# The head of a fused state-space and gated-FFN kernel: factors over 128 partitions, two load queues, row tiles normalised one by one

## The chip, the cores and the metric

The kernel runs on one core of one Trainium2 chip, as one launch. The metric is device time in microseconds. The engines are TensorE (PE; its weight loads are PEld), VectorE (DVE), ScalarE (ACT), GpSimd (POOL) and SyncE (SP), which here only issues transfers.

## The reference, cut to what matters

```python
x  = L0_attn_u                        # (2, 1024, 512): 2048 rows of 512, float32
xn = layernorm(x)                     # over the 512, eps 1e-5
s  = causal_conv(xn, K) + D * xn      # K: 512 taps from the S4 parameters (a small chain of complex work)
def lora_linear(x, w, a, b):          # rank 16
    return x @ w.T + (x @ a.T) @ b.T * 2.0
h1 = lora_linear(xn, w1, A1, B1)      # 1376 hidden units
h3 = lora_linear(xn, w3, A3, B3)
g  = silu(lora_linear(silu(h1) * h3, w2, A2, B2))
out = x + s * g
```

## The kernel before

**Tiling.** The 2048 rows are four blocks of 512. For each block the 1376 hidden units are 11 tiles (`HT`) of up to 128; each tile j has three places: "gate" (h1), "up" (h3) and "down" (the product with w2 for tile j - 1). The weights stay in SBUF. In the first block each weight tile must first be made: it is loaded (`load_raw`), the rank-16 product of the factors is formed on PE into a spare bank (`fold`), DVE adds it (`fold_add`), ACT rounds the sum to the high part (`fold_hi`) and DVE or POOL subtracts to give the low part (`fold_lo`; the list `POOL_LO` says which tiles are POOL's). Every matrix product is three matmuls on high and low parts (`three`, lines 819 to 821).

**The head.** Before tile 1 of the first block, four row tiles of 128 rows are loaded into `xn`, their mean and variance are formed on DVE (`rows_moments`, lines 671 and 674), scale and shift on POOL (`rows_rstd`, two row tiles at a time), applied on ACT (`rows_norm`, line 559), turned on PE (`turn_rows`, line 814) and split by ACT and DVE (`rows_hi`, `rows_lo`, lines 533 and 678). Tile 0's h1 and h3 are made in halves of 256 rows, since the first two row tiles are ready first: `start()` on PE holds that order, with the first five folds (`FOLD_FIRST`) in between, and `keep_busy` matmuls on a cleared tile that give nothing. The first factors come as `lr`, 16 partitions by 2176 columns. All factors are also loaded as `spread` (128 partitions by 708), split by ACT and POOL and stored by six transfers as a stack of 48 rows over 128 partitions, which the folds from `(1, 2)` on read.

**What sets the order.** All engines run hand-written instruction lists in order; waits on semaphores join them. All loads are on SP's queue. The spare banks alternate between folds, and a fold waits until DVE has read the bank's last one. After the head, PE's list for tile 1 begins with `wait_group(pe, 1, 1)` and its first matmul waits for nothing else than the gate's Silu. The fold of `(1, 2)`, behind the gate of tile 1, is the first to read the stack.

**Names.** `g_cleared` releases the idle matmuls; `lora_in` the first fold; `xhi_done` and `xlo_done` count split row tiles; `whi_done`, `wlo_done` and `wlo_pool` count split weights; `h1_ready` and `h3_ready` end a tile's two sums.

Of the kernel before, what the change touches and what calls it, by code (L numbers as in the profile page):

```python
# [119 lines left out]
STACK_STEP = P // R  # L120
PLAIN = {1: 1, 3: 1, 2: 0}
# [21 lines left out]
POOL_LO = [(3, 1), (1, 3), (3, 3), (3, 4)]  # L143
# [77 lines left out]
def build(nc, x, xT, w1, w3, w2, lora, lora_st, lora_mv, s4_lanes, s4_vc, s4_bp, s4_scalars, trig, lanes, dft, outT):  # L221
    ctx = ExitStack()
    with ctx:
# [34 lines left out]
        small = put("small", [P, 4])  # L258
        bvec = put("bvec", [P, 2])
# [11 lines left out]
        lr = at("lora_first", [R, LORA_FIRST], W13_AT[1, 7])  # L271
# [56 lines left out]
        eps_added, rstd_ready, shift_step, shift_ready = map(sem, ("eps_added", "rstd_ready", "shift_step", "shift_ready"))  # L328
        xn_ready, xt_turned = sem("xn_ready"), sem("xt_turned")
# [88 lines left out]
        def _(sync):  # L418
# [10 lines left out]
            def store_scales(b):  # L429

                sync.wait_ge(shift_ready, (b + 1) * (RT // 2))
                sync.dma_start(scales_dram[:, :].rearrange("k (p r) -> p k r", r=RT), scales[:, :, :]) \
                    .then_inc(scales_stored, 16)
# [32 lines left out]
            sync.dma_start(lr[:, :], lora).then_inc(lora_in, 16)  # L466
            load_tile(1)
            sync.dma_start(lane_c[:, :], lanes).then_inc(const_in, 16)
            load_raw(1, 0)
            load_tile(2)  # L470
# [53 lines left out]
        def _(act):  # L524
# [32 lines left out]
            def rows_norm(r):  # L557
                act.wait_ge(shift_ready, r // 2 + 1)
                nc.scalar.activation(xn[:, r, :], xn[:, r, :], ACT.Identity, bias=scales[:, 1, r:r + 1],
                                     scale=scales[:, 0, r:r + 1]).then_inc(xn_ready, 1)  # L560
# [49 lines left out]

            act.wait_ge(g_cleared, 1)
# [4 lines left out]
            rows_norm(1)  # L616
            fold_hi(1, 0)
            rows_hi(0)
            rows_hi(1)
            rows_norm(2)  # L620
            rows_norm(3)
            fold_hi(3, 0)
            rows_hi(2)
            rows_hi(3)
            act.wait_ge(spread_in, 32)
            nc.scalar.copy(spread_hl[:, 0, :], spread[:, :]).then_inc(spread_hi, 1)
            fold_hi(1, 1)
            hidden(0, 0)
# [13 lines left out]
        def _(dve):  # L642
# [114 lines left out]

            nc.vector.memset(g[:, 0:P], 0.0).then_inc(g_cleared, 1)
            rows_moments(0, 0)
            rows_moments(0, 1)  # L760
            rows_moments(0, 2)
            fold_add(1, 0)
            rows_moments(0, 3)
            fold_lo(1, 0)
            rows_lo(0)
            rows_lo(1)
            fold_add(3, 0)
            fold_lo(3, 0)
            rows_lo(2)
            rows_lo(3)  # L770
            fold_add(1, 1)
            fold_lo(1, 1)
            fold_add(3, 1)
            fold_lo(3, 1)
            hidden_mul(0, 0)
            fold_add(2, 0)
            fold_lo(2, 0)
            body(0, 0, 1, True, False)
# [6 lines left out]
        def _(pe):  # L785
# [51 lines left out]
            def start():  # L837


                lo, hi = slice(0, BLK // 2), slice(BLK // 2, BLK)  # L840
                pe.wait_ge(g_cleared, 1)
                keep_busy(7)
                pe.wait_ge(lora_in, 16)
                fold(1, 0)
                fold(3, 0)
                keep_busy(1)
                pe.wait_ge(const_in, 16)
                turn_rows(0)
                turn_rows(1)
                keep_busy(2)  # L850

                pe.wait_ge(whi_done, 1)
                pe.wait_ge(xhi_done, RT // 2)
                for c in range(DC):
                    pe.matmul(h1[:, lo], w13_tile(1, 0, 0)[:, c, :], xt[:, 0, 0, c, lo], start=(c == 0), stop=False)
                wait_split(pe, 1, 0)
# [18 lines left out]
                mm.then_inc(b_ready, 1)  # L875

# [102 lines left out]
        def _(pool):  # L979
# [46 lines left out]
            pool.wait_ge(spread_hi, 1)  # L1026
            tt(spread_hl[:, 1, :], spread[:, :], spread_hl[:, 0, :].bitcast(F32), ALU.subtract).then_inc(spread_lo, 1)
            pool.wait_ge(spread_lo, 1)
            fold_lo(3, 1)
# [14 lines left out]
            for kind, j in POOL_LO[1:]:  # L1044
# [145 lines left out]
```

## Time and profile before

| | us |
|---|---|
| median of 3 runs | 423.31 (422.84 to 423.36) |
| the profiled execution | 423.09 |
| its span, first to last instruction | 421.3 |
| head, until tile 1 starts on PE | 23.37 |
| PE busy | 413.7 |

A busy PE isn't a PE at its peak: in the first 13 us a matmul of 128 float32 columns follows the last after 0.24 us, later after 0.13. The granted-clock column of the windows reads 1.00 in these first 13 us too, so the rate there is read from the spacing of matmuls. A PE matmul of plain float32 shows as two records, one of the rounded type as one.

### The profile page before, as it was taken

To read this page: it belongs to the slowest core of one execution; us is meant where nothing else is said; L and a number is where in the kernel's file an instruction comes from. 1 tells how busy PE (TensorE), PEld (TensorE's weight loads), DVE (VectorE), ACT (ScalarE), POOL (GpSimd) and SP (SyncE) were. 2 spreads that over 40 slices of the span, in tenths; PEclk is the share of its full clock that TensorE was granted. 3 is DMA by queue.
4 is the path that set the end of the run, shared out by engine and by line. 5 is a ranking of instruction groups with operands and counts; after the bars stand their busy time and mean duration, and the time that the engine had idled before them with its cause. 6 is when DMAs were issued, how large, how long until landed. Compare 5 with 4: busy or idle time off the path is not lost.

```text
span 421.3 us, 5027 instructions
## 1 busy us (share of the span) xinstructions
PE 413.7 (98%) x1868; PEld 343.7 (82%) x1868; DVE 159.6 (38%) x245; ACT 102.6 (24%) x168; POOL 67.0 (16%) x131
## 2 busy tenths in 40 slices
PE   8999999999999999999999999999999999999995
PEld 7977888887888888888888888888888888888883
DVE  4658686655485221224135222132324111111115
ACT  6543322333242111122112111212212111111111
POOL 3246734344220103200000101400000000000000
PEclk9999999999999999999999999999999999999999
DMA  8474832321506201000004301000002000000002
GB/s 275 120 219 128 300 98 74 90 82 25 157 14 211 88 2 50 2 0 0 2 23 149 128 0 50 0 0 0 0 0 100 0 0 0 0 0 0 0 0 100
DMA packets 14063, 26.19 MB, mean 62 GB/s; under 512 B 2480, under 2 KB 4208, under 8 KB 14032
## 3 DMA queue, kind: packets, MB, share of 16 engines
q1 hardware_dynamic: 13888, 25.41, 19.3%
q0 software_dynamic: 160, 0.59, 0.4%
q8 instruction: 8, 0.13, 0.1%
q14 instruction: 7, 0.06, 0.1%
HBM read 20.37 MB, written 4.53 MB: 59 GB/s over the span
## 4 chain that ended last, share of the span: by engine, by line
PE 94%; DVE 2%; issue 1%; DMA 1%; ACT 1%; SPq 0%; DVEq 0%; ACTq 0%
PE h L819 20%; PE h L821 20%; PE h L820 20%; PE f L819 9%; PE f L821 9%; PE f L820 9%; PE spare L806 2%; DMA lora_first<-lora_dram 1%; DVE w L662 1%; PE spare L801 1%; PE f L814 1%; DVE gate L711 0%; PE spare L821 0%; PE spare L819 0%; PE spare L820 0%
## 5 line engine op out<-in xcount | busy, mean ns | idle before, releaser
L819 PE MATMUL h<-xt,w 128*128 (+2 forms) x356 | 138.3, 388 | 0.2 <-DVE w L662 0.2
L820 PE MATMUL h<-xt,w 128*128 (+2 forms) x356 | 137.5, 386 | 0.0
L821 PE MATMUL h<-xt,w 128*128 (+2 forms) x356 | 137.5, 386 | 0.0
L819 PEld LDWEIGHTS h<-xt,w 128*128 128x128 f32 x356 | 66.9, 188 | 13.9 <-DVE w L662 0.6
L698 DVE TENSOR_TENSOR g<-g,h 128x512 f32<-128x512 f32 x44 | 30.2, 687 | 126.4 <-PE h L821 126.4
L821 PEld LDWEIGHTS h<-xt,w 128*128 128x128 f32 x356 | 66.9, 188 | 13.5
L820 PEld LDWEIGHTS h<-xt,w 128*128 128x128 f32 x356 | 66.9, 188 | 13.2
L703 DVE TENSOR_TENSOR ghl<-g,ghl 128x512 fp32r<-128x512 f32 x44 | 32.4, 736 | 98.6 <-ACT ghl L555 98.5
L819 PE MATMUL f<-ghl,w2f 128*128 128x512 f32 x176 | 68.7, 390 | 0.0
L820 PE MATMUL f<-ghl,w2f 128*128 128x512 f32 x176 | 68.6, 390 | 0.0
L821 PE MATMUL f<-ghl,w2f 128*128 128x512 f32 x176 | 68.6, 390 | 0.0
L555 ACT CAST ghl<-g 128x512 fp32r<-128x512 f32 x44 | 27.3, 621 | 166.4 <-PE f L821 157.4
L545 ACT ACTIVATE g<-h 128x512 f32<-128x512 f32 x44 | 26.3, 598 | 52.9 <-PE h L821 52.8
L821 PEld LDWEIGHTS f<-ghl,w2f 128*128 128x128 f32 x176 | 33.1, 188 | 6.9
L819 PEld LDWEIGHTS f<-ghl,w2f 128*128 128x128 f32 x176 | 33.1, 188 | 6.6
L820 PEld LDWEIGHTS f<-ghl,w2f 128*128 128x128 f32 x176 | 33.1, 188 | 6.6
L652 DVE SCALAR_TENSOR_TENSOR raw<-spare,raw 128x512 f32<-128x512 f32 (+2 forms) x33 | 22.3, 676 | 3.8 <-PE spare L806 2.8
L992 POOL TENSOR_TENSOR scales<-moments,lane_c 128x2 f32<-128x2 f32 x8 | 1.9, 242 | 126.7 <-DVE moments L674 126.7
L529 ACT CAST w<-raw 128x512 fp32r<-128x512 f32 (+1 forms) x22 | 13.4, 611 | 32.8 <-DVE raw L652 32.8
L992 POOL TENSOR_TENSOR normal_rows<-xres,scale_rows 128x512 f32 (+1 forms) x12 | 15.1, 1290 | 20.5 <-DMA scale_rows<-scales_scratch 20.5
L662 DVE TENSOR_TENSOR w<-raw,w 128x512 fp32r<-128x512 f32 (+1 forms) x18 | 15.3, 848 | 2.0 <-ACT w L529 1.9
L568 ACT ACTIVATE gate<-f 128x512 f32<-128x512 f32 x16 | 9.5, 597 | 21.5 <-PE f L821 17.5
(105 smaller groups left out, 274.3 us busy)
## 6 DMA issues: line engine op xcount, KB each, us to landing
raw<-w_dram SPq DMA_DIRECT2D x28, 256.0 KB, 3.4
xres<-xT_dram SPq DMA_DIRECT2D x4, 1024.0 KB, 7.1
outT_dram<-xres SPq DMA_DIRECT2D x16, 256.0 KB, 2.4
rows_next<-x_dram SPq DMA_DIRECT2D x4, 512.0 KB, 3.8
scale_rows<-scales_scratch SPq DMA_DIRECT2D x3, 512.0 KB, 3.9
xn<-x_dram SPq DMA_DIRECT2D x4, 256.0 KB, 3.8
rows<-x_dram SPq DMA_DIRECT2D x2, 512.0 KB, 7.5
raw<-w_dram SPq DMA_DIRECT2D x4, 224.0 KB, 2.5
```

The lines of the kernel that those rows point to most:

```text
L529: nc.scalar.copy(folded(kind, j, 0), raw_tile(kind, j)).then_inc(whi_done, 1)
L545: nc.scalar.activation(g[:, :], h1[:, :], ACT.Silu).then_inc(silu_done, 1)
L555: nc.scalar.copy(ghl[:, 0, :], g[:, :]).then_inc(ghi_done, 1)
L568: nc.scalar.activation(gate[:, n % 2, :], f[c][:, :], ACT.Silu).then_inc(gate_done, 1)
L652: nc.vector.scalar_tensor_tensor(out=rt, in0=low, scalar=LORA_SCALE, in1=rt, op0=ALU.mult, op1=ALU.add) \
L662: nc.vector.tensor_tensor(folded(kind, j, 1), raw_tile(kind, j), folded(kind, j, 0).bitcast(F32), ALU.subtract).then_inc(wlo_done, 1)
L698: nc.vector.tensor_tensor(g[:, :], g[:, :], h3[:, :], ALU.mult).then_inc(g_done, 1)
L703: nc.vector.tensor_tensor(ghl[:, 1, :], g[:, :], ghl[:, 0, :].bitcast(F32), ALU.subtract).then_inc(glo_done, 1)
L819: pe.matmul(out, w[1], m[0], start=start, stop=False)
L820: pe.matmul(out, w[0], m[1], start=False, stop=False)
L821: return pe.matmul(out, w[0], m[0], start=False, stop=stop)
L992: return nc.gpsimd.tensor_tensor(out, a, c, op)
```

## The change

1. `lr` gets 128 partitions. The 16 factor rows go to every eighth of them (`STACK_STEP` is 8), and the rest is cleared ahead of the load: DVE clears 1216 columns, POOL 960. SP waits for both before it issues this load. The first folds have 128 contraction rows, 112 of them zero.
2. `g`, which the idle matmuls read, is cleared by POOL and no longer by DVE. There are 11 idle matmuls at the start, not 7, and none later (3 before).
3. Row tiles 1 and 2 are loaded from ACT's queue, ahead of ACT's table load. SP's queue now begins row tile 0, weight (1, 0), factors, constants, row tile 3.
4. In the first block DVE adds epsilon for each row tile and POOL forms scale (a power) and shift (one instruction) singly; `rows_norm(r)` waits for its own tile. It was four POOL instructions for a pair.
5. The low part of `spread` and of weight (3, 1) goes from POOL to DVE.
6. The lists of PE, DVE and ACT in the head are put in another order. The folds of (1, 1), (3, 1) and (2, 0) come before the second half of tile 0.

```diff
-        lr = at("lora_first", [R, LORA_FIRST], W13_AT[1, 7])
+        lr = at("lora_first", [P, LORA_FIRST], W13_AT[1, 7])
...
             load_tile(0)
-            sync.dma_start(lr[:, :], lora).then_inc(lora_in, 16)
-            load_tile(1)
+            load_raw(1, 0)
+            sync.wait_ge(factors_dve, 1)
+            sync.wait_ge(factors_pool, 1)
+            sync.dma_start(lr[0:P:STACK_STEP, :], lora).then_inc(lora_in, 16)
             sync.dma_start(lane_c[:, :], lanes).then_inc(const_in, 16)
-            load_raw(1, 0)
-            load_tile(2)
             load_tile(3)
...
             def rows_norm(r):
-                act.wait_ge(shift_ready, r // 2 + 1)
+                act.wait_ge(first_shift, r + 1)
...
+            for r in (1, 2):
+                act.dma_start(xn[:, r, :], x[r * P:(r + 1) * P, :]).then_inc(x_in[r], 16)
...
+            def rows_first(r):
+                rows_moments(0, r)
+                dve.wait_ge(moments_ready, r + 1)
+                nc.vector.tensor_scalar(scales[:, 0, r:r + 1], moments[:, r, 1:2], EPS, None, ALU.add).then_inc(first_eps, 1)
...
-            nc.vector.memset(g[:, 0:P], 0.0).then_inc(g_cleared, 1)
+            nc.vector.memset(lr[:, 0:FACTORS_BY_DVE], 0.0).then_inc(factors_dve, 1)
...
+            nc.gpsimd.memset(g[:, 0:P], 0.0).then_inc(g_cleared, 1)
+            pool.wait_ge(g_cleared, 1)
+            nc.gpsimd.memset(lr[:, FACTORS_BY_DVE:LORA_FIRST], 0.0).then_inc(factors_pool, 1)
...
+            for r in range(RT):
+                pool.wait_ge(first_eps, r + 1)
+                tt(scales[:, 0, r:r + 1], scales[:, 0, r:r + 1], half[:, :], ALU.pow).then_inc(first_rstd, 1)
+                pool.wait_ge(first_rstd, r + 1)
+                nc.gpsimd.tensor_scalar(scales[:, 1, r:r + 1], moments[:, r, 0:1], scales[:, 0, r:r + 1], -1.0,
+                                        ALU.mult, ALU.mult).then_inc(first_shift, 1)
```

PE's list in the head before, from the first fold to the end of tile 0 (`spare` is a fold's bank, `f` the turned rows, `h` a sum of tile 0 or an idle matmul):

```order
L806 MATMUL spare<-lora_first 128x128 [waits lora_in]
L806 MATMUL spare<-lora_first 128x128 x7
L835 MATMUL h<-g 128x128
L814 MATMUL f<-lane_c,xn 128x128 [waits xn_ready,const_in]
...
L835 MATMUL h<-g 128x128 x2
L855 MATMUL h<-xt,w_49 128x256 [waits xhi_done,whi_done]
L855 MATMUL h<-xt,w_49 128x256 x3
L859 MATMUL h<-xt,w_49 128x256 [waits xlo_done,wlo_done]
...
L806 MATMUL spare<-lora_first 128x128 [waits spare_free0]
L806 MATMUL spare<-lora_first 128x128 x3
L819 MATMUL h<-xt,w_49 128x256 [waits xlo_done]
```

And now (line numbers of the changed kernel):

```order
L821 MATMUL spare<-lora_first 128x128 [waits lora_in]
L821 MATMUL spare<-lora_first 128x128 x3
L829 MATMUL f<-lane_c,xn 128x128 [waits xn_ready,const_in]
L829 MATMUL f<-lane_c,xn 128x128 x3
L821 MATMUL spare<-lora_first 128x128 x4
...
L821 MATMUL spare<-lora_first 128x128 [waits spare_free0]
L821 MATMUL spare<-lora_first 128x128 x3
L869 MATMUL h<-xt,w_49 128x256 [waits xhi_done,whi_done]
L869 MATMUL h<-xt,w_49 128x256 x3
L821 MATMUL spare<-lora_first 128x128 [waits spare_free1]
L821 MATMUL spare<-lora_first 128x128 x3
L874 MATMUL h<-xt,w_49 128x256 [waits xlo_done,wlo_done]
```

The folds of (1, 1) and (3, 1), which stood behind the first halves, stand around the four matmuls that need only high parts.

DVE's list in the head before, from the first fold's addition on:

```order
L652 SCALAR_TENSOR_TENSOR raw<-spare,raw 128x512 [waits fold_ready,raw_in0]
L671 BN_STATS stats<-xn 128x6 [waits fold_added,x_in3]
L674 BN_AGGR moments<-stats 128x2 [waits stats_done]
L662 TENSOR_TENSOR w_49<-raw,w_49 128x512 [waits whi_done]
L678 TENSOR_TENSOR xt<-f,xt 128x4x128 [waits xhi_done] x2
L652 SCALAR_TENSOR_TENSOR raw<-spare,raw 128x512 [waits fold_ready,raw_in4]
L662 TENSOR_TENSOR w_49<-raw,w_49 128x512 [waits fold_added,whi_done]
L678 TENSOR_TENSOR xt<-f,xt 128x4x128 [waits xhi_done] x2
```

And now:

```order
L658 SCALAR_TENSOR_TENSOR raw<-spare,raw 128x512 [waits fold_ready,raw_in4]
L690 TENSOR_TENSOR xt<-f,xt 128x4x128 [waits fold_added,xhi_done]
L668 TENSOR_TENSOR w_49<-raw,w_49 128x512 [waits whi_done]
L690 TENSOR_TENSOR xt<-f,xt 128x4x128 [waits xhi_done]
L781 TENSOR_TENSOR lora_spread_split<-lora_spread,lora_spread_split 128x708 [waits spread_hi]
L668 TENSOR_TENSOR w_49<-raw,w_49 128x512 [waits whi_done]
L658 SCALAR_TENSOR_TENSOR raw<-spare,raw 128x512 [waits fold_ready,raw_in1]
L658 SCALAR_TENSOR_TENSOR raw<-spare,raw 128x512 [waits fold_added,fold_ready,raw_in5]
L690 TENSOR_TENSOR xt<-f,xt 128x4x128 [waits fold_added,xhi_done]
L690 TENSOR_TENSOR xt<-f,xt 128x4x128 [waits xhi_done]
```

Between the first and the second pair of row tiles (the lines with `xt<-f,xt`) DVE now has the low part of `spread` and the additions of (1, 1) and (3, 1).

## Rows read from the trace of the kernel before

**Rows 1.** The page, part 1: busy time of each engine, share of the span

```profile
PE 413.7 (98%) x1868; PEld 343.7 (82%) x1868; DVE 159.6 (38%) x245; ACT 102.6 (24%) x168; POOL 67.0 (16%) x131
```

**Rows 2.** Waits of PE from 13 us on: line, releaser, total, times, longest

```profile
PE spare L806 <- DVEq L656: 0.4, 1, 0.4
PE h L819 <- DVE w L662: 0.2, 1, 0.2
```

**Rows 3.** Timeline of the head, PE: start, us, engine, line, operation, count

```profile
1.06 3.36 PE L835 MATMUL h<-g 128*128 128x128 f32 x14 [1.06 <-DVE g L758]
5.08 3.77 PE L806 MATMUL spare<-lora_first 16*128 16x128 f32 x16 [0.66 <-DMA lora_first<-lora_dram]
8.78 0.80 PE L835 MATMUL h<-g 128*128 128x128 f32 x2
12.05 1.15 PE L855 MATMUL h<-xt,w 128*128 128x256 f32 x4
13.03 0.28 PE L859 MATMUL h<-xt,w 128*128 128x256 f32 x1
13.15 0.28 PE L860 MATMUL h<-xt,w 128*128 128x256 f32 x1
16.38 1.15 PE L806 MATMUL spare<-lora_first 16*128 16x128 f32 x8
17.47 0.39 PE L819 MATMUL h<-xt,w 128*128 128x256 f32 x1
22.83 0.60 PE L874 MATMUL spare<-bp_sb,vc_sb 64*128 64x1 f32 x4
23.37 0.50 PE L819 MATMUL h<-xt,w 128*128 128x512 f32 x1
```

**Rows 4.** Timeline of the head, memsets and the factors' load; the load in the chain

```profile
0.84 0.17 DVE L758 MEMSET g<- 128x128 f32 x1 [0.84 <-PEq L1183]
0.74 2.10 POOL L1015 MEMSET lora_stack<- 128x2400 f32 x1 [0.29 <-POOLq L1183]
1.19 3.84 DMA lora_first<-lora_dram
```

**Rows 5.** Timeline of the head, DVE, POOL and ACT

```profile
4.11 0.69 DVE L671 BATCH_NORM_STATS2 stats<-xn 128x6 f32<-128x512 f32 x1 [3.11 <-DMA xn<-x_dram]
9.56 0.18 DVE L674 BATCH_NORM_AGGREGATE moments<-stats 128x2 f32<-128x6 f32 x1 [0.15 <-DVE stats L671]
7.88 0.69 DVE L652 SCALAR_TENSOR_TENSOR raw<-spare,raw 128x512 f32<-128x512 f32 x1
8.71 0.69 DVE L671 BATCH_NORM_STATS2 stats<-xn 128x6 f32<-128x512 f32 x1
15.25 1.29 DVE L678 TENSOR_TENSOR xt<-f,xt 128x512 fp32r<-128x512 f32 x2 [0.64 <-ACT xt L533]
8.21 1.52 ACT L559 ACTIVATE xn<-xn,scales 128x512 f32<-128x512 f32 x2 [3.18 <-POOL scales L992]
23.52 0.58 POOL L992 TENSOR_TENSOR small<-lane_c,small 128x1 f32<-128x1 f32 x1
16.46 1.70 POOL L992 TENSOR_TENSOR lora_spread_split<-lora_spread,lora_spread_split 128x708 fp32r<-128x708 f32 x1 [5.11 <-ACT lora_spread_split L626]
```

**Rows 6.** Windows: busy of each engine, granted clock, DMA share, GB/s

```profile
2.00:3.00 1.00, 1.00 (x7) 1.00 (x6) 0.00 (x0) 0.99 (x3) 0.83 (x1) 1.00 1.06 363
3.00:4.00 1.00, 1.00 (x7) 1.00 (x6) 0.00 (x0) 1.00 (x1) 0.00 (x0) 1.00 1.01 129
```

**Rows 7.** Timeline at 30 us: a POOL and a DVE instruction at one time

```profile
30.18 1.30 POOL L992 TENSOR_TENSOR den_im<-den_im,res 128x512 f32<-128x512 f32 x1 [5.01 <-ACT res L588]
30.30 1.73 DVE L662 TENSOR_TENSOR w<-raw,w 128x512 fp32r<-128x512 f32 x1
```

**Rows 8.** Windows at the end, behind the last matmul (columns as in rows 6)

```profile
418.00:419.00 1.00, 0.00 (x0) 0.00 (x0) 0.46 (x1) 0.00 (x0) 0.00 (x0) 1.00 0.57 219
419.00:420.00 1.00, 0.00 (x0) 0.00 (x0) 0.00 (x0) 0.00 (x0) 0.00 (x0) 0.60 0.66 258
```

More of the change, by code:

```diff
@@ L120 @@
 STACK_STEP = P // R
+FACTORS_BY_DVE = 1216
 PLAIN = {1: 1, 3: 1, 2: 0}
@@ L142 @@
 FOLD_NO = {f: n for n, f in enumerate(FOLDS)}
-POOL_LO = [(3, 1), (1, 3), (3, 3), (3, 4)]
+POOL_LO = [(1, 3), (3, 3), (3, 4)]
 DVE_LO = [f for f in FOLDS if f not in POOL_LO]
@@ L258, in build @@
         small = put("small", [P, 4])
+        half = put("half", [P, 1])
         bvec = put("bvec", [P, 2])
@@ L328, in build @@
         eps_added, rstd_ready, shift_step, shift_ready = map(sem, ("eps_added", "rstd_ready", "shift_step", "shift_ready"))
+        first_eps, first_rstd, first_shift = sem("first_eps"), sem("first_rstd"), sem("first_shift")
+        half_set, factors_dve, factors_pool = sem("half_set"), sem("factors_dve"), sem("factors_pool")
         xn_ready, xt_turned = sem("xn_ready"), sem("xt_turned")
@@ L429, in store_scales @@
             def store_scales(b):
-                sync.wait_ge(shift_ready, (b + 1) * (RT // 2))
+                sync.wait_ge(shift_ready, b * (RT // 2))
                 sync.dma_start(scales_dram[:, :].rearrange("k (p r) -> p k r", r=RT), scales[:, :, :]) \
@@ L616, in _ @@
             rows_norm(1)
+            rows_hi(0)
             fold_hi(1, 0)
-            rows_hi(0)
             rows_hi(1)
+            fold_hi(3, 0)
+            act.wait_ge(spread_in, 32)
+            nc.scalar.copy(spread_hl[:, 0, :], spread[:, :]).then_inc(spread_hi, 1)
             rows_norm(2)
             rows_norm(3)
-            fold_hi(3, 0)
             rows_hi(2)
+            fold_hi(1, 1)
             rows_hi(3)
[L625 to L628, printed above, removed]
             fold_hi(3, 1)
             fold_hi(2, 0)
+            hidden(0, 0)
             act.wait_ge(b_ready, 1)
@@ L756, in body @@
                 out_sum(b, par)
-            nc.vector.memset(g[:, 0:P], 0.0).then_inc(g_cleared, 1)
-            rows_moments(0, 0)
-            rows_moments(0, 1)
-            rows_moments(0, 2)
+            nc.vector.memset(lr[:, 0:FACTORS_BY_DVE], 0.0).then_inc(factors_dve, 1)
+            rows_first(0)
+            rows_first(1)
+            rows_first(2)
             fold_add(1, 0)
-            rows_moments(0, 3)
+            rows_first(3)
+            fold_add(3, 0)
+            rows_lo(0)
             fold_lo(1, 0)
-            rows_lo(0)
             rows_lo(1)
-            fold_add(3, 0)
+            dve.wait_ge(spread_hi, 1)
+            nc.vector.tensor_tensor(spread_hl[:, 1, :], spread[:, :], spread_hl[:, 0, :].bitcast(F32), ALU.subtract) \
+                .then_inc(spread_lo, 1)
             fold_lo(3, 0)
+            fold_add(1, 1)
+            fold_add(3, 1)
             rows_lo(2)
             rows_lo(3)
-            fold_add(1, 1)
             fold_lo(1, 1)
-            fold_add(3, 1)
             fold_lo(3, 1)
-            hidden_mul(0, 0)
             fold_add(2, 0)
             fold_lo(2, 0)
+            hidden_mul(0, 0)
             body(0, 0, 1, True, False)
@@ L841, in start @@
                 pe.wait_ge(g_cleared, 1)
-                keep_busy(7)
+                keep_busy(11)
                 pe.wait_ge(lora_in, 16)
                 fold(1, 0)
-                fold(3, 0)
-                keep_busy(1)
                 pe.wait_ge(const_in, 16)
                 turn_rows(0)
+                fold(3, 0)
                 turn_rows(1)
-                keep_busy(2)
+                fold(1, 1)
                 pe.wait_ge(whi_done, 1)
@@ L855, in start @@
                     pe.matmul(h1[:, lo], w13_tile(1, 0, 0)[:, c, :], xt[:, 0, 0, c, lo], start=(c == 0), stop=False)
+                fold(3, 1)
                 wait_split(pe, 1, 0)
@@ L864, in start @@
                 hidden(0, 0, 0, 3, h3, lo)
-                fold(1, 1)
+                fold(2, 0)
                 pe.wait_ge(xlo_done, RT)
                 hidden(0, 0, 0, 1, h1, hi).then_inc(h1_ready, 1)
-                fold(3, 1)
-                hidden(0, 0, 0, 3, h3, hi).then_inc(h3_ready, 1)
-                fold(2, 0)
                 bankt = take(0, ("B",), True)
@@ L875, in start @@
                 mm.then_inc(b_ready, 1)
+                hidden(0, 0, 0, 3, h3, hi).then_inc(h3_ready, 1)
             def down_wait(b, j):
@@ L994, in rows_rstd @@
             def rows_rstd(b, r):
-                two, n = slice(r, r + 2), b * (RT // 2) + r // 2 + 1
+                two, n = slice(r, r + 2), (b - 1) * (RT // 2) + r // 2 + 1
                 pool.wait_ge(moments_ready, b * RT + r + 2)
@@ L1013, in next_scale @@
                     tt(xnt[:, par, 1, c, :], resid(par, c), scale_rows[:, 0, :], ALU.mult).then_inc(scaled, 1)
+            nc.gpsimd.memset(g[:, 0:P], 0.0).then_inc(g_cleared, 1)
+            pool.wait_ge(g_cleared, 1)
+            nc.gpsimd.memset(lr[:, FACTORS_BY_DVE:LORA_FIRST], 0.0).then_inc(factors_pool, 1)
+            pool.wait_ge(factors_pool, 1)
             nc.gpsimd.memset(lst[:, 0:ST_COLS].bitcast(F32), 0.0).then_inc(stack_cleared, 1)
+            nc.gpsimd.memset(half[:, :], -0.5).then_inc(half_set, 1)
+            pool.wait_ge(half_set, 1)
+            for r in range(RT):
[4 more added lines that the diff above has]
+                                        ALU.mult, ALU.mult).then_inc(first_shift, 1)
+                pool.wait_ge(first_shift, r + 1)
             pool.wait_ge(const_in, 16)
-            for r in range(0, RT, 2):
-                rows_rstd(0, r)
             def fold_lo(kind, j):
@@ L1024, in fold_lo @@
                 pool.wait_ge(wlo_pool, POOL_LO.index((kind, j)) + 1)
[L1026 to L1029, printed above, removed]
             pool.wait_ge(s4_in, 16 * 3)
@@ L1043, in _ @@
             tt(mag[:, :], mag[:, :], res[:, :], ALU.add).then_inc(mag_ready, 1)
-            for kind, j in POOL_LO[1:]:
+            for kind, j in POOL_LO:
                 fold_lo(kind, j)
```

## Prediction

> **What bounds the kernel now.** The page's first part puts PE at 98% of the span [rows 1]. The list of PE's waits shows what is left to win behind the head: from 13 us to the end two short waits, 0.6 us together [rows 2]. So behind the head the time is the length of PE's own list, which the change leaves alone. The kernel can only get shorter by letting tile 1 start on PE before 23.37 us (the last of [rows 3]), or by upsetting what follows.
>
> In the head's timeline the reader is to see three things. First, PE is slow until about 13 us: 16 records of the first two folds take 3.77 us, 0.236 us each, while eight of the same shape take 1.15 us at 16.38; the float32-rounded matmuls at 12.05 go at about 0.24 us each, and the one at 13.03 is followed by the next after 0.12 [rows 3]. That is TensorE at 1.2 and then at 2.4 GHz. Before the change of rate PE had run idle matmuls from 1.06, stood 0.7 us, run the folds of 16 contraction rows from 5.08, and run full-height work without a pause from 8.78. Second, although PE is called busy, much of what it does before 12 us is filling. Third, from 17.47 (upper half of h1) to 23.37 PE's list holds two half sums, the three folds (3, 1), (2, 0) and "B": everything real, nothing hidden.
>
> **The change part by part.** PE's work between the second group of the lower half (13.03, L859) and tile 1 takes 10.34 us now (23.37 - 13.03). The change takes the folds (1, 1) and (3, 1) out of it and puts them ahead of that group, where PE waits for others. A fold there costs eight records plus the switch to and from it: 16.38 to 17.47 is 1.09 us [rows 3]. So 10.34 - 2 x 1.09 = 8.16 us remain. Fold (2, 0) stays in the stretch, moved from behind the last sum to the middle: no gain, unless PE waits there for DVE anyway. What decides is when that group can start, and when the upper half can.
>
> Both hang on DVE's list, and I add it up from the arrival of row tile 0, now at 4.11 us after an idle time of 3.11 [rows 5].
> - A row tile: statistics 0.69, pause 0.15, aggregate 0.18, pause 0.15 [rows 5], and the new addition of epsilon. No row shows a DVE instruction on 128 x 1. Its cost lies between 0 and the aggregate's 0.18; the aggregate and the memset of 128 columns (0.17) [rows 4] are nearest, so I take 0.15. Sum 1.32, four times: 5.3 us. Before, a tile cost 1.02.
> - Two fold additions ahead of the group, each 0.83 to the next instruction (7.88 to 8.71): 1.7 us [rows 5].
> - Low parts of row tile 0, weight (1, 0), row tile 1, about 0.65 each (1.29 for two): 1.9 us.
> So the group starts at 4.1 + 8.9 = 13.0, and 0.1 later on PE: as before. DVE was idle for loads in this stretch and is now filled with single-tile work. Normalising singly buys nothing here by itself; it only keeps ACT and PE ahead. Check of these: epsilon 0 is there at 5.4, the power takes 0.58 [rows 5], the shift about as much as another small POOL step (0.2), so ACT normalises at about 6.4 where it now starts at 8.21, 0.76 a tile; both tiles are turned and rounded by about 10.5, before DVE asks for the second at 12.4. A shift of 1 us there is hidden.
> - Behind the group DVE has the low part of `spread` (708/512 x 0.69 = 0.95), weight (3, 0) 0.65, two additions 1.66, two row tiles 1.29: 4.55 us. The upper half can start at 13.0 + 4.6 = 17.6 us. PE on its side has the group, eight turns, the lower half of h3 and fold (2, 0): now 13.03 to 16.38 is 3.35, plus 1.09, so 17.5 us. The two are level; now it is 17.47.
> - From there PE has h1, "B" and h3 in place of h1, (3, 1), h3, (2, 0), "B". Now 17.47 to 23.37 is 5.90. Minus two folds, 2.2, is 3.7. Tile 1 starts at 17.6 + 3.7 = 21.3. **The gain is 23.37 - 21.3 = 2.0 us**, from two folds that have moved under DVE's time.
>
> **Whether the covers hold.** The factors' load waits for both memsets. POOL's rate is 2.10/2400 us a column, so g and 960 columns end at 0.74 + 0.11 + 0.84, about 1.9 with a pause. DVE's is bounded by 0.17 for 128 columns above (1.6 us) and by one fixed part of about 0.1 below (0.7); I take 1.2, so issue at about 2.1. With the 3.84 us of now [rows 4] the factors land at 6.0, where 11 idle matmuls (22 records at 0.24 from 1.1) end at 6.4. Fold (1, 0) then takes at most 0.95 and DVE wants it at 8.1: 0.7 us to spare. Moving POOL's low parts to DVE costs DVE 0.95 and 0.69, the first counted above, the second behind the row tiles, where DVE has been idle between folds. It gives back POOL's 1.70 and its late end at 18.16 [rows 5], so the six stack transfers start some 4 us sooner; that isn't late now (fold (1, 2) does not wait) [rows 2], so I count nothing, but with tile 1 2 us sooner it is needed. ACT's Silu of tile 0 waits behind its cast of weight (2, 0), for which DVE needs three more instructions after the last row tile: 17.6 + 2.0, the cast and the Silu 0.6 each, 20.8: half a microsecond ahead of tile 1 at 21.3.
>
> The window 3:4 shows a DMA share of 1.01 at 129 GB/s, against 363 a window before [rows 6]: the factors' 16 long rows clog the engines. Spread over the partitions this should ease. The Trainium skill ("SBUF — State Buffer", Door 1: the DMA port swizzle) maps partitions to 16 write ports; by its formula rows 0 to 15 reach four ports, every eighth partition eight. The row agrees in kind.
>
> Two queues don't add bandwidth where the share is already 1.0 [rows 6]. Row tile 0 now shares with row tile 1 from the start: up to 256 KB at 363 GB/s, 0.7 us, may come ahead of its end. Then every DVE time above moves by 0.7 and the gain is 1.3. I keep 4.1 for the sum, since lighter factors work the other way, and 4.8 for the range. The Trainium skill ("DMA: Bandwidth & Descriptors", on issuing from several engines) says that this saves only the issue time, since all queues run on the same 16 engines and interleave. By that rule alone the gain would be the 1.3.
>
> **Rivals.** (a) **The clock isn't up when the real work starts.** For: PE has pauses of about 0.7 us ahead of the four high-part matmuls and 1.4 us behind the fold that follows them, with the later idle matmuls gone; and it took 4.2 us of full-height work from 8.78 before [rows 3]. Against: the first 6 us are now solid full-height work, and at the end of the span the granted clock still reads 1.00 in 418 to 419, a window without a single matmul, and falls only in 419 to 420 [rows 8], so a pause of 1.4 us alone doesn't bring it down. Price: if the rate comes up only some 4 us after 13.1, work of 2 us has taken 4, so 2.0 is lost: no change, 423.3; if it is down for a part of this, 422.3.
> (b) **The factors come late.** They now wait for two memsets and queue behind 1 MB of other loads. Each microsecond past 6.8 us moves DVE's chain, all of it. It makes the kernel measurably slower from a landing at 9.7 on (6.8 + 2.0 + 0.85), and at 10 it costs 3.2: 424.5. Speaking against: the load takes 3.84 now [rows 4], and would need 7.9.
> (c) **DVE's terms are shorter.** Consecutive instructions overlap by up to 0.08 and epsilon may be nearly free; 20 instructions give 1 us or so, and PE's own list then binds; with high parts ready sooner it reaches the upper half at 16.9. Also POOL now clashes less with DVE: a low part on DVE took 1.73 us, 0.69 alone, beside POOL's 1.30 [rows 7]; and this stall, part of the 0.6 us of waits [rows 2], may fall otherwise. Gain 3.3: 420.0.
> (d) **What the head wins is given back.** At 30 to 37 us DVE is the one PE waits for, and its order there is as before, triggered by PE; so nothing for it but a new clash like that one [rows 7], 1 us: gain 1.0, 422.3.
>
> **How the numbers follow.** The sum is made against the profiled execution, 423.09 (span 421.3, 1.8 around it): 421.1. The median is 423.31, so **421.3**. Its own range is 420.5 (terms shorter by 0.8) to 422.1 (row tile 0 late by 0.7). Chances: forecast 0.62; (a) 0.14; (b) 0.06; (c) 0.10; (d) 0.08. A measurement of this kernel tells 0.2% from no change, 0.85 us. Faster takes the forecast 0.62, (c) 0.10, of (d) 0.05 and of (a) 0.02: 0.79. Within 0.2%: 0.10 of (a) and 0.03 of (d), 0.13. Slower: (b) 0.06 and what of (a) runs on past 2 us, 0.02. The range 420.1 to 423.0 leaves out (b), the worst of (a) and the end of (c).
>
> **What the changed profile would show.** Tile 1's first matmul at 21.3 (20.5 to 22.1). Records of the folds at 0.13 us spacing before 10 us, and L874 at 0.12. Row tile 0's statistics at 4.1 to 4.8. DVE without idle time above 0.3 us from there to the last row tile; L874 starting within 0.3 of 13.1. The two waits behind the head as before [rows 2]. The sum is wrong if DVE waits for `fold_ready` at its first addition, if L874's spacing is 0.24, or if tile 1 starts at 21.3 and the span has not shrunk by 2.

## The result, and the profile after

| | before | changed |
|---|---|---|
| median | 423.30 us | 419.88 us (419.76 to 420.03) |
| ratio to before, 95% interval | | 0.9919 (0.9905 to 0.9934) |
| profiled execution, its span | 423.09, 421.3 | 420.03, 418.2 |
| tile 1 starts on PE | 23.37 | 20.36 |
| from there to the end of the span | 397.9 | 397.8 |

The forecast was 421.3 with a range of 420.1 to 423.0. The kernel became faster, as forecast, but by 3.4 us and not by 2.0, so the time lies below the range. In the profiled executions the difference is 3.1 us, of which 3.0 are in the head (before tile 1 starts on PE) and 0.1 behind it.

PE's timeline of the changed kernel, the head (start, us, engine, line, operation, shape, count, idle time before and its releaser); it answers to [rows 3]:

```profile
0.99 4.35 PE L850 MATMUL h<-g 128*128 128x128 f32 x22 [0.99 <-POOL g L1028]
6.25 1.16 PE L821 MATMUL spare<-lora_first 128*128 128x128 f32 x8 [0.90 <-DMA lora_first<-lora_dram]
...
10.50 1.05 PE L821 MATMUL spare<-lora_first 128*128 128x128 f32 x8
12.39 0.36 PE L874 MATMUL h<-xt,w 128*128 128x256 f32 x1 [0.83 <-DVE xt L690]
...
15.71 1.02 PE L816 MATMUL spare<-lora_first 128*128 128x512 f32 x2
16.66 0.39 PE L834 MATMUL h<-xt,w 128*128 128x256 f32 x1
...
20.36 0.40 PE L834 MATMUL h<-xt,w 128*128 128x512 f32 x1
```

The 22 idle records take 4.35 us. At the 0.236 us a record of [rows 3] they would take 5.2, so TensorE came to 2.4 GHz among them. The first fold's eight records take 1.16 us, so it runs at 2.4 GHz from its start. The low-part group (L874) starts at 12.39, the upper half at 16.66.

DVE's timeline of the same stretch, which answers to [rows 5]:

```profile
3.95 0.69 DVE L677 BATCH_NORM_STATS2 stats<-xn 128x6 f32<-128x512 f32 x1 [1.81 <-DMA xn<-x_dram]
4.79 0.18 DVE L680 BATCH_NORM_AGGREGATE moments<-stats 128x2 f32<-128x6 f32 x1
5.00 0.15 DVE L686 TENSOR_SCALAR scales<-moments 128x1 f32<-128x1 f32 x1
5.08 0.68 DVE L677 BATCH_NORM_STATS2 stats<-xn 128x6 f32<-128x512 f32 x1
...
7.24 0.15 DVE L686 TENSOR_SCALAR scales<-moments 128x1 f32<-128x1 f32 x1
7.52 0.69 DVE L658 SCALAR_TENSOR_TENSOR raw<-spare,raw 128x512 f32<-128x512 f32 x1
8.36 0.69 DVE L677 BATCH_NORM_STATS2 stats<-xn 128x6 f32<-128x512 f32 x1
...
9.42 0.15 DVE L686 TENSOR_SCALAR scales<-moments 128x1 f32<-128x1 f32 x1
9.51 0.69 DVE L658 SCALAR_TENSOR_TENSOR raw<-spare,raw 128x512 f32<-128x512 f32 x1
...
11.55 0.69 DVE L690 TENSOR_TENSOR xt<-f,xt 128x512 fp32r<-128x512 f32 x1
12.15 0.89 DVE L781 TENSOR_TENSOR lora_spread_split<-lora_spread,lora_spread_split 128x708 fp32r<-128x708 f32 x1
...
15.32 1.29 DVE L690 TENSOR_TENSOR xt<-f,xt 128x512 fp32r<-128x512 f32 x2 [0.15 <-DVE raw L658]
```

DVE goes from 3.95 to 16.6 us nearly without a pause. From the start of one row tile's statistics to the start of the next are 1.11 to 1.13 us. One small wait is there: the second fold addition starts 0.09 us after the start of the epsilon ahead of it (9.42, 9.51), the first 0.28 us (7.24, 7.52), so VectorE stood about 0.2 us for the first fold. The waits of PE from 13 us on are those of [rows 2], to a tenth:

```profile
PE spare L821 <- DVEq L662: 0.4, 1, 0.4
PE h L834 <- DVE w L668: 0.2, 1, 0.2
```

### The profile page after: what moved, and what is told of

Same layout as the page of the kernel before. It is cut to its first block, busy times and chain, and to the rows that moved or that the text cites. A ratio compares the mean times of both kernels' runs of the same rounds, so it can differ in the third digit from the quotient of the medians.

```text
span 418.2 us, 5041 instructions
## 1 busy us (share of the span) xinstructions
PE 409.6 (98%) x1870; PEld 340.2 (81%) x1870; DVE 161.3 (39%) x251; ACT 102.5 (25%) x168; POOL 65.9 (16%) x132
## 4 chain that ended last, share of the span: by engine, by line
PE 93%; DVE 3%; issue 1%; DMA 1%; ACT 1%; DVEq 0%; ACTq 0%
PE h L834 20%; PE h L835 20%; PE h L836 20%; PE f L834 9%; PE f L835 9%; PE f L836 9%; PE spare L821 1%; DVE w L668 1%; DMA lora_first<-lora_dram 1%; DVE raw L658 1%; PE spare L816 1%; DVE gate L723 1%; PE spare L834 0%; PE spare L835 0%; PE spare L836 0%
## 5 line engine op out<-in xcount | busy, mean ns | idle before, releaser
L572 ACT ACTIVATE gate<-f 128x512 f32<-128x512 f32 x16 | 9.5, 598 | 21.4 <-PE f L836 19.0
```

Of the source, the lines that this page charges most:

```text
L572: nc.scalar.activation(gate[:, n % 2, :], f[c][:, :], ACT.Silu).then_inc(gate_done, 1)
```

## The experiments

Theories: **D**, the head is bounded by VectorE's list, with PE's own list level behind it, and the clock only has to be up in time (the forecast's view of the bound). **C**, it is the clock that pays, and the full height of the folds decides it. **L**, the loads pay. Rivals for a single run have letters of their own in its expectation. Each run gives two numbers. One is the median, with its ratio to the kernel before that ran beside it (423.39 beside e1 to e4, 423.78 beside the others). The other is where tile 1 starts on PE, in one profiled execution. That execution lies 0.3 us below its kernel's median in e2 and e7 and 0.7 below in e11, 0.3 above in e1 and 0.7 above in e5.

| run | median | ratio (95%) | tile 1 | span less tile 1 |
|---|---|---|---|---|
| changed | 419.88 | 0.9919 (0.9905 to 0.9934) | 20.36 | 397.8 |
| e1 | 427.12 | 1.0074 (1.0051 to 1.0098) | 27.70 | 397.9 |
| e2 | 421.15 | 0.9949 (0.9932 to 0.9966) | 21.19 | 397.8 |
| e3 | 421.35 | 0.9958 (0.9941 to 0.9975) | 21.52 | 398.0 |
| e4 | 429.07 | 1.0129 (1.0112 to 1.0146) | 29.59 | 397.8 |
| e5 | 421.06 | 0.9937 (0.9920 to 0.9953) | 22.04 | 397.9 |
| e6 | 420.25 | 0.9920 (0.9906 to 0.9935) | 20.58 | 397.8 |
| e7 | 419.97 | 0.9915 (0.9898 to 0.9931) | 20.06 | 397.8 |
| e8 | 420.63 | 0.9927 (0.9911 to 0.9944) | 21.04 | 397.9 |
| e9 | 420.98 | 0.9936 (0.9922 to 0.9951) | 21.28 | 397.8 |
| e10 | 422.99 | 0.9985 (0.9976 to 0.9995) | 23.21 | 398.1 |
| e11 | 424.39 | 1.0017 (1.0008 to 1.0026) | 24.05 | 397.9 |
| e12 | 419.91 | 0.9920 (0.9904 to 0.9936) | 20.26 | 398.0 |

The last column settles where to look: over a spread of 9.5 us at tile 1 it stays within 0.3 us. Nothing of the head is given back later, and nothing is won there.

### Factors and order, each undone alone

**e1**, the factors in 16 partitions:

```diff
-        lr = at("lora_first", [P, LORA_FIRST], W13_AT[1, 7])
+        lr = at("lora_first", [R, LORA_FIRST], W13_AT[1, 7])
...
-            sync.wait_ge(factors_dve, 1)
-            sync.wait_ge(factors_pool, 1)
-            sync.dma_start(lr[0:P:STACK_STEP, :], lora).then_inc(lora_in, 16)
+            sync.dma_start(lr[:, :], lora).then_inc(lora_in, 16)
```

The two memsets of `lr` go as well.

> The changed kernel, but the first factors stay in 16 partitions: no clearing, no wait for it, the load issued at once. Tile 1 starts on PE at 20.36 us in the changed kernel. Theory D (VectorE's list and PE's own list set the head, the high clock only has to be there by 12 us): in the changed kernel the idle matmuls reach 2.4 GHz before the first fold, at about 4.3 us, so 16-row folds change nothing: tile 1 at 20.1 to 20.5, median within 0.4 us of 419.9. Rival C (full-height folds are what keeps the clock up): the folds run at 0.24 us a record again, the group of low parts starts at 1.2 GHz, tile 1 at 21.4 or later, median 421 or more. Rival L (16 long rows clog the load engines): row tile 1 or 2 lands later and VectorE waits for it, 0.5 to 1 us at tile 1.

Measured: 427.12 us, 7.2 above the changed kernel and slower than the kernel before. Windows of e1 (stretch, its length, busy and count of PE, PEld, DVE, ACT, POOL, granted clock, DMA share, GB/s):

```profile
6.00:7.00 1.00, 0.00 (x0) 0.00 (x0) 0.88 (x3) 0.55 (x1) 0.70 (x3) 1.00 0.99 256
7.00:8.00 1.00, 0.84 (x7) 0.84 (x8) 0.39 (x3) 0.69 (x2) 0.72 (x3) 0.97 1.06 394
8.00:9.00 1.00, 1.00 (x6) 0.78 (x6) 0.32 (x1) 0.39 (x1) 0.53 (x2) 0.50 1.08 388
...
20.00:21.00 1.00, 1.00 (x7) 1.00 (x6) 0.00 (x0) 0.30 (x1) 0.00 (x0) 0.50 1.18 215
21.00:22.00 1.00, 1.00 (x8) 1.00 (x7) 0.68 (x1) 1.00 (x3) 0.00 (x0) 0.71 1.01 191
```

The granted clock falls from 1.00 to 0.50 at 8 us and comes back between 21 and 22: 1.2 GHz for 13 us. PE's timeline shows it as the length of a fold, 1.40 for the first, 2.07 for the next:

```profile
7.16 1.40 PE L818 MATMUL spare<-lora_first 16*128 16x128 f32 x8 [1.78 <-DMA lora_first<-lora_dram]
8.49 1.11 PE L826 MATMUL f<-lane_c,xn 128*128 128x128 f32 x4
9.53 2.07 PE L818 MATMUL spare<-lora_first 16*128 16x128 f32 x8
```

Theory C's bounds hold (tile 1 at 21.4 or later, 421 or more), but it doesn't give the size, and no other theory does. L has a part: issued at 1.65 and not 2.16, the load lands 5.5 us later at 7.1, against 4.0 us and 6.2 in the changed kernel. The Trainium skill ("SBUF — State Buffer", Door 1: the DMA port swizzle) would have rows 0 to 15 reach four write ports and every eighth partition eight; the trace agrees that the second form lands sooner, but two things differ between the runs (form and moment of issue), so the ports alone aren't shown. One doubt stays: e1 also has a pause of 1.78 us before the fold.

**e11** closes that pause:

```diff
-                keep_busy(11)
+                keep_busy(18)
```

> The kernel of e1 (first factors in 16 partitions, all else as changed) with 18 idle matmuls and not 11, so that full-height work goes on without a pause until the factors land near 7.2 us. Theory H (16-row matmuls don't hold the clock): the granted clock falls to 0.5 during the three 16-row folds all the same, tile 1 at 25 us or later, median 424.3 or more. Rival G (in e1 it was the pause of 1.8 us that let it fall): the clock stays at 1.00, VectorE is only late by the factors' landing, tile 1 at 21.5, median 421.1.

Measured: 424.39, tile 1 at 24.05. Theory H asked for a median of 424.3 or more and tile 1 at 25 or later. The median is there, the profiled tile 1 isn't, but this execution took 423.69, 0.7 less than the median. Its mean granted clock was 0.994, that of the nine others 0.990 to 0.992, from which the low stretch was longer in them. Windows of e11, columns as above:

```profile
12.00:13.00 1.00, 1.00 (x9) 0.88 (x8) 0.85 (x3) 1.00 (x3) 0.41 (x2) 1.00 0.95 344
13.00:14.00 1.00, 1.00 (x9) 0.87 (x8) 1.00 (x2) 1.00 (x2) 0.17 (x1) 0.98 0.18 70
14.00:15.00 1.00, 1.00 (x6) 0.78 (x5) 1.00 (x3) 0.84 (x2) 0.92 (x2) 0.50 0.00 0
```

PE is busy 1.00 of every window here, and the clock falls all the same, at 14 us, in the fourth of the 16-row folds that stand among turns and products of full height. It is up again between 17 and 18 us (0.81 in that window). The changed kernel runs the same folds at full height, with two pauses, and doesn't fall. So these 16-row folds don't hold the clock, even without a pause. Rival G, the pause, is out as the only cause. Why e1 fell 6 us sooner and stayed low four times as long is open. Its four executions are alike (mean granted clock 0.982 to 0.987), so it isn't chance. The pause is the main thing that differs from e11, but that it does this is not shown.

**e2**, only 7 idle matmuls (`keep_busy(7)` for 11):

> The changed kernel with 7 idle matmuls at the start, not 11. Theory D: PE stands from 4.4 to 6.2 us, and the clock is up somewhat later but before 12 us: tile 1 at 20.3 to 20.6, median within 0.4 us of 419.9. Rival C: the clock comes up only behind a stretch of solid work from 6.2 on, so folds and turns run at half rate and the first high-part group ends after 12.4: tile 1 at 21 or later, median 420.6 or more.

Measured: 421.15, 1.3 more than the changed kernel. PE stood from 4.35 to 6.02 and the clock wasn't up yet:

```profile
6.02 2.08 PE L821 MATMUL spare<-lora_first 128*128 128x128 f32 x8 [1.67 <-DMA lora_first<-lora_dram]
```

VectorE then waited 0.80 us for the first fold and everything behind moved by it: group at 13.21, tile 1 at 21.19. C's time is met and D's isn't, although the clock was up well before 12 us, as D had it (the second fold takes 1.48, the third 1.06). The four more idle matmuls are worth 0.8 us at tile 1 (1.3 by the medians), because the first fold is on VectorE's path.

**e3**, the lists of PE, VectorE and ScalarE in the old order, all else as changed. Of PE's:

```diff
                 fold(1, 0)
+                fold(3, 0)
                 pe.wait_ge(const_in, 16)
                 turn_rows(0)
-                fold(3, 0)
                 turn_rows(1)
-                fold(1, 1)
```

> The changed kernel with the lists of PE, VectorE and ScalarE in the order of the kernel before (the low part of the spread factors on VectorE behind row tile 3, no idle matmuls in the middle). Theory D, adding up with the durations of the changed trace: VectorE lets the low-part group start at 11.5, PE then has all of its list, folds (1,1), (3,1), (2,0) included: tile 1 at 21.6, 1.2 us later than in the changed kernel, median 421.1. If the order alone is what pays (the forecast's view), tile 1 is at 22.4 or later, median 421.9 or more. If the clock alone pays, no difference from 419.9.

Measured: 421.35, tile 1 at 21.52; expected by D, with durations of the changed trace, 421.1 and 21.6. The low-part group starts at 11.96, later than D's 11.5 but sooner than in the changed kernel; the folds (1, 1) and (3, 1) are back behind it in PE's list (at 15.38 and 17.71). So the new order is worth 1.2 us at tile 1 here (1.5 by the medians), and the rest of the change 1.85.

**e4**, only the new lists, in the kernel before:

> The kernel before with only the new lists of PE, VectorE and ScalarE (factors in 16 partitions, 7 idle matmuls, loads on one queue, scale and shift in pairs, low parts on GpSimd). The forecast's view (two folds moved under VectorE's time, all else hidden): nearly all of the gain, tile 1 at 21.4, median 421.2. Theory D: row tiles are loaded as late as before and the clock comes up late, so folds and turns run at half rate ahead of the group: tile 1 at 22.3 to 23, median 422.2 to 423. Rival C: no gain at all, 423.3.

Measured: 429.07, slower than before by 5.7 us. No theory had that; the forecast's view had 421.2. PE's timeline:

```profile
5.58 1.15 PE L806 MATMUL spare<-lora_first 16*128 16x128 f32 x8 [1.33 <-DMA lora_first<-lora_dram]
9.64 1.09 PE L814 MATMUL f<-lane_c,xn 128*128 128x128 f32 x4 [2.92 <-ACT xn L559]
10.66 2.07 PE L806 MATMUL spare<-lora_first 16*128 16x128 f32 x8
```

and two windows of it, columns as above:

```profile
12.00:15.00 3.00, 3.00 (x14) 2.44 (x14) 2.01 (x4) 1.19 (x3) 0.00 (x0) 0.50 0.55 184
21.00:24.00 3.00, 3.00 (x16) 3.00 (x15) 1.24 (x2) 2.11 (x4) 0.00 (x0) 0.50 1.08 224
```

Here PE runs the first fold at 2.4 GHz (1.15), but waits 2.9 us for the first normalised tile, and the clock falls in that wait (granted clock 0.67 in the window from 7 to 8 us, 0.50 behind it). More 16-row folds stand between the turns and ahead of the group, and the clock is 0.50 until 24 us. How much of this is the wait's and how much the folds', no run tells.

**e10**, only the factors on 128 partitions, in the kernel before (VectorE clears `g` and 1216 columns, GpSimd 960, the load behind row tiles 0 and 1):

```diff
+            load_tile(1)
+            sync.wait_ge(factors_dve, 1)
+            sync.wait_ge(factors_pool, 1)
+            sync.dma_start(lr[0:P:STACK_STEP, :], lora).then_inc(lora_in, 16)
```

> The kernel before with one part of the change: the first factors on every eighth of 128 cleared partitions (VectorE and GpSimd clear, SyncE waits, the load stands behind row tiles 0 and 1); 7 idle matmuls, lists of before, all loads on one queue. Theory C (the height of the folds decides whether TensorE comes to 2.4 GHz): the rate comes up at about 9.5 us, not 13.0, though the folds start 1 us later; the turns and idle matmuls run at 0.13 us a record, the low-part group starts at 12.0 to 12.5, tile 1 at 22.3 to 22.8, median 422.2 to 422.8. Theory D (VectorE's list decides, the clock is no matter): the factors' load is later, so nothing is won, tile 1 at 23.4 or later, median 423.3 or more.

Measured: 422.99, ratio 0.9985; tile 1 at 23.21. The clock is up by 5.24 (16 records of folds in 2.05 us, against 3.77 in [rows 3]), much sooner than C asked for. Yet in the profiled pair the head gains 0.16 us, since in the old order PE then waits 1.5 us for ScalarE and 0.6 for low parts, and row tile 2's statistics start at 7.91, 1.0 later than in the kernel before. Neither theory's numbers came: C had tile 1 at 22.8 at most, D 23.4 or more. By the medians the gain is 0.8 us (0.2 to 1.0 by the interval). So a high clock on a list that waits is worth little.

The two kernels, run side by side, say one thing more of the clock. The mean granted clock of an execution was 0.990 to 0.992 in 6 of 13 of the kernel before, and 0.997 or more in all ten of e10. In all 48 executions of the ten kernels with full-height folds it was never below 0.993, in e1 never above 0.987. A mean near 1.00 by itself shows little, since the column reads 1.00 ahead of a first recorded fall: two of e4's four executions read 0.999 and 1.00 and were within 0.8 us as slow as the two at 0.98.

### What VectorE's list costs

**e8** puts one instruction more on it:

```diff
+            nc.vector.memset(tz[:, :], 0.0).then_inc(extra, 1)
             fold_add(3, 0)
             rows_lo(0)
```

> The changed kernel with one more instruction on VectorE, a memset of 512 columns of a tile not yet in use, between row tile 3's statistics and the second fold addition: some 0.45 us by the rate of the 1216-column memset (1.07 us). Theory D: every microsecond on this list is one at the start of tile 1: group at 12.85, tile 1 at 20.8, median 420.3. Rival P (slack of PE): tile 1 later by less than 0.2.

Measured: 420.63, tile 1 at 21.04, 0.68 later. From the first fold addition to the second are 2.52 us and not 1.99, so the memset costs 0.5 of the list. The first addition was itself 0.2 later: in this execution 22 idle records took 5.06 us, not 4.35, and the clock came up only within the first fold (1.50 us for its eight records, not 1.16). Both delays went through in full; theory P (slack of PE) is out.

**e7** takes epsilon off it:

```diff
-                dve.wait_ge(moments_ready, r + 1)
-                nc.vector.tensor_scalar(scales[:, 0, r:r + 1], moments[:, r, 1:2], EPS, None, ALU.add).then_inc(first_eps, 1)
...
+                pool.wait_ge(moments_ready, r + 1)
+                ts(scales[:, 0, r:r + 1], moments[:, r, 1:2], EPS, ALU.add).then_inc(first_eps, 1)
```

> The changed kernel with epsilon added by GpSimd (one more small instruction per row tile there) and not by VectorE. The trace of the changed kernel shows 0.11 us per row tile for it on VectorE's list (1.13 between starts against 1.02 before). Theory D: the low-part group starts 0.4 us earlier, at 11.95, the upper half at 16.2, tile 1 at 19.9 to 20.0, median 419.5. Rival P (PE's own list binds the upper half already): the group starts earlier but tile 1 stays at 20.3 or more.

Measured: 419.97, tile 1 at 20.06. Row tiles come 0.91 us apart, but VectorE then stands for the fold:

```profile
7.42 0.69 DVE L658 SCALAR_TENSOR_TENSOR raw<-spare,raw 128x512 f32<-128x512 f32 x1 [0.56 <-PE spare L819]
```

So it wins 0.3 us at tile 1 and nothing that the medians can tell. This lies between D (19.9 to 20.0, 419.5) and P (20.3 or more): VectorE's saving ends in a wait for the first fold. **e12** keeps epsilon on GpSimd and puts the factors' load ahead of the weight's in SyncE's queue:

```diff
-            load_raw(1, 0)
             sync.wait_ge(factors_dve, 1)
             sync.wait_ge(factors_pool, 1)
             sync.dma_start(lr[0:P:STACK_STEP, :], lora).then_inc(lora_in, 16)
+            load_raw(1, 0)
```

> A try at a faster kernel: epsilon on GpSimd (as e7) and the factors' load ahead of the one of weight (1,0) in SyncE's queue. In e7 VectorE waited 0.56 us for the first fold, since the factors landed at 6.1. With 256 KB less ahead of them they should land 0.3 to 0.6 us sooner. Theory D: that wait goes, the group starts at 11.6, tile 1 at 19.5, median 419.4. Rival: the landing doesn't move, since the load is issued at 2.16 either way and shares the DMA engines with row tiles 1 and 2: tile 1 at 20.0, median 419.9.

Measured: 419.91, tile 1 at 20.26. The load takes 3.3 us and not 4.0 and lands at 5.5, but the 22 idle records took 5.06 us here and PE began the fold only at 5.85; VectorE still waits 0.36 for the fold, and 0.54 for row tile 3, which now lands later. The rival's numbers came, but not its reason: the landing did move. Neither e7 nor e12 is better than the changed kernel by more than the intervals.

### The other parts undone

**e5**, all loads on SyncE's queue:

```diff
-            for r in (1, 2):
-                act.dma_start(xn[:, r, :], x[r * P:(r + 1) * P, :]).then_inc(x_in[r], 16)
```

> The changed kernel with row tiles 1 and 2 loaded from SyncE's queue (order: row tiles 0 and 1, weight (1,0), factors, constants, row tiles 2 and 3). Row tile 2 is then issued near 3.4 us and lands at 6.9 to 8, VectorE wants it at 6.2. Theory D (VectorE's list is the bound of the head): all behind it moves by that wait, tile 1 at 21.1 to 22, median 420.6 to 421.6. Rival (the second queue is no gain, the DMA engines being full anyway): within 0.3 us of 419.9.

Measured: 421.06, tile 1 at 22.04.

```profile
3.57 0.69 DVE L677 BATCH_NORM_STATS2 stats<-xn 128x6 f32<-128x512 f32 x1 [1.43 <-DMA xn<-x_dram]
8.06 0.69 DVE L677 BATCH_NORM_STATS2 stats<-xn 128x6 f32<-128x512 f32 x1 [2.17 <-DMA xn<-x_dram]
```

Row tile 0 is here 0.4 us sooner than with two queues, row tile 2's statistics start 1.9 later (6.19 there) and VectorE stands for 2.17. To be rid of that wait is what the second queue buys: 1.7 us at tile 1 in this execution, and 1.2 us by the medians. The Trainium skill's statement ("DMA: Bandwidth & Descriptors", Issuing engines are not separate DMA queues) is that the queues share the DMA engines and that issuing from several saves only issue time. Both rows agree in kind: with two queues tile 0, which shares, comes 0.4 later, and tile 2, issued at 1.2 and not at 3.5, comes sooner. The 0.4 is not fixed, since with one queue in the kernel before tile 0 came at 4.11 [rows 5].

**e6**, both low parts on GpSimd as before. This list moves weight (3, 1); the instruction for `spread` is moved as well:

```diff
-POOL_LO = [(1, 3), (3, 3), (3, 4)]
+POOL_LO = [(3, 1), (1, 3), (3, 3), (3, 4)]
```

> The changed kernel with the low parts of the spread factors and of weight (3,1) on GpSimd again. Theory D (VectorE's list is the bound up to the upper half): 0.8 us less ahead of row tiles 2 and 3 on VectorE, but GpSimd's instruction of 1.7 us stands from 11.5 to 13.2 beside VectorE's low part of weight (3,0), which then takes 1.7 and not 0.7: the upper half and tile 1 where they are, 20.2 to 20.6, median within 0.4 us of 419.9. If there is no clash, theory P (PE's list ends at 16.6 too): no difference either. The forecast's count (0.95 and 0.69 us more on VectorE, all on its list) would give 0.9 us of gain, tile 1 at 19.5, median 419.0. Slower than 420.5 only if fold (1,2) waits for the stack.

Measured: 420.25, tile 1 at 20.58, inside D's 20.2 to 20.6. The clash is there: beside GpSimd's 1.70 VectorE's instruction takes 1.80 and not 0.69, as in [rows 7].

```profile
11.61 1.70 POOL L1002 TENSOR_TENSOR lora_spread_split<-lora_spread,lora_spread_split 128x708 fp32r<-128x708 f32 x1 [1.07 <-ACT lora_spread_split L628]
12.06 1.80 DVE L668 TENSOR_TENSOR w<-raw,w 128x512 fp32r<-128x512 f32 x1
```

So moving the low part of `spread` off GpSimd costs VectorE 0.8 us of its list and saves it 1.1.

**e9**, scale and shift in pairs (the old `rows_rstd` on GpSimd, no epsilon on VectorE, `rows_norm` waits for its pair):

> The changed kernel with scale and shift formed for two row tiles at a time on GpSimd, four instructions a pair, and no epsilon on VectorE. The forecast's statement (normalising singly buys nothing by itself): tile 1 at 20.0 to 20.4, the 0.45 us saved on VectorE included, median 419.5 to 419.9. Rival N (it does): GpSimd's chain of 1.5 us starts behind the second row tile's moments and the constants, ScalarE normalises row tile 0 at 8.3 and not 6.3, the second row tile is rounded near 11.5, the group starts at 12.8 or later, tile 1 at 20.7 to 21.3, median 420.3 to 420.9.

Measured: 420.98, tile 1 at 21.28. Row tile 0 is normalised from 7.85 and not 6.28, and the late turns hold the fold (3, 0) back, for which VectorE waits 1.19 us:

```profile
10.44 0.69 DVE L658 SCALAR_TENSOR_TENSOR raw<-spare,raw 128x512 f32<-128x512 f32 x1 [1.19 <-PE spare L819]
```

The forecast's "buys nothing here by itself" is wrong: single tiles buy 0.9 us, with the 0.4 that epsilon costs already paid.

## Why the prediction was wrong

- **What bounds the kernel.** Right. PE's list behind the head is the same length in fourteen kernels, and the two waits behind the head stayed.
- **The row tiles on VectorE: the term that failed.** "Sum 1.32, four times: 5.3 us" counted pauses and durations one behind the other. Measured: 1.13 from start to start, since the addition of epsilon starts 0.21 after the aggregate's start, and the next statistics 0.08 after that. Four times 0.19 is 0.76 us. Row tile 0 came at 3.95, not 4.1 (0.15), the low parts took 1.8 and not 1.9, and the wait of 0.2 for the first fold goes the other way. Together VectorE was through with the group's parts at 12.15, where the forecast had 13.0. The group started on PE at 12.39, where it had 13.1.
- **The upper half.** Predicted 17.6, measured 16.66: the same 0.85, and 0.1 less on VectorE behind the group (4.5 for 4.6). That VectorE (16.6) and PE (fold until 16.6) are level there was right.
- **The last stretch.** 3.7 predicted, 3.70 measured (16.66 to 20.36).
- **So tile 1** is at 20.36 instead of 21.3, and the head is 3.0 us shorter and not 2.0. The median moved 0.4 more than the profiled pair, which is less than the kernel before differs from itself (422.84 to 423.36); the interval, 2.8 to 4.0 us, holds both. Rival (c), "DVE's terms are shorter", is what came: it named the overlap of consecutive instructions, put the upper half at 16.9 and the time at 420.0, and had a chance of 0.10. A sum made of overlapping small instructions was given its upper end as the middle.
- **What gains.** The forecast put the whole gain on two folds that move. By e3 the new order is worth 1.2 us at tile 1 with the rest in place, by e4 it costs 6.2 without. The rest is worth 1.85 in the old order (e3). "Normalising singly buys nothing" fell with e9 (0.9). The two queues count 1.2 by the medians of e5, and the forecast took them as a risk of 0.7 only: it expected row tile 0 between 4.1 and 4.8, and it came at 3.95.
- **The clock.** Rival (a) named the pauses as the danger and priced it at 2.0. The pauses were 0.9 and 0.8 us long and did no harm, nor did one of 1.39 in e3 or one of 1.54 in e9. What lets the clock fall without any pause is 16-row work (e11: 4.5 us over the changed kernel by the medians, a part of it for the later landing, as VectorE waits 1.65 us for the first fold there). With a pause ahead of the folds, and the later landing of that load included, the price is 7.3 us at tile 1 (e1). The forecast read "16 contraction rows" in [rows 3] and didn't ask what they do to a clock that is already up.
- **The covers.** The factors landed at 6.2 (6.0 said), but VectorE, being quicker, asked for the first fold at 7.3 and not at 8.1. The forecast let that fold take "at most 0.95"; its own row has 1.15 for eight records, and it took 1.16. (Nor does its bound of 6.8 us for the landing follow: 8.1 less 0.95 is 7.15.) So the cover fell short by 0.2, where the forecast had 0.7 to spare, and its own sign of being wrong, VectorE waiting at its first addition, was there in small. In e2, e3, e7, e8, e9 and e12 that wait was 0.30 to 0.80 us. Only the wait came, though: rival (b)'s late landing did not.

## What to carry to other kernels

When an order is tight, each part of a change can be worth its price only with the others: here the order alone loses 5.7 us, the spread factors alone win 0.8, all parts together win 3.4. For a chain of short instructions take the spacing between starts, and not durations plus pauses, from a place in a trace where such instructions follow each other. Where no row has it, let the range cover every instruction of the chain overlapping with the next. Matmuls of few contraction rows ahead of real work can cost more than their own time. Here, filling up with zero rows cost PE nothing (at 2.4 GHz 1.15 us a fold with 16 rows, 1.05 to 1.16 with 128), and the clock stayed up.

## What the runs showed of the hardware

- Eight records of a 16-row fold take 1.15 us at 2.4 GHz, and of a full-height one 1.05 to 1.16: the same. But the granted clock falls among the 16-row folds: at 8 us in e1, at 14 us in e11, there with PE busy in every window. In e1 it stayed at 0.50 of full for 13 us although turns and products of full height ran among the folds.
- The moment of the rise differs between executions and kernels with the same 22 idle records: they took 4.26 (e9) to 5.06 us (e8, e12).
- The granted-clock column reads 1.00 ahead of its first recorded fall, also where spacings show 1.2 GHz at the start; falls and rises after that (e1, e4, e11) agree with the spacings.
- 16 rows of 8704 bytes into 16 neighbouring partitions landed 5.5 and 5.9 us after their issue (e1, e11), into every eighth partition 3.3 to 4.5 us (e12, changed, e3). With a single queue it was 3.84 in neighbouring partitions, issued at 1.19 [rows 4], and 2.9 and 3.5 in every eighth, issued at 2.3 and 2.2 (e10, e5). So what else is in flight counts too.
- A memset of 1216 columns takes 1.07 us on VectorE, one of 512 columns 0.48; a power on 128 x 1 takes 0.55 on GpSimd.
